# Adding the last chunk's rows to the token tiles: by an accumulating DMA in DRAM, or by 0/1 products on TensorE

## The reference, cut to what matters

```python
flat = layernorm(x)                      # 1250 x 1024
for e in range(8):
    cw = sum(where(topk_idx == e, topk_w, 0))
    y = gelu(flat @ w1[e].T + b1[e]) @ w2[e].T + b2[e]
    out = out + y * cw[:, None]          # only tokens that chose e have cw != 0
out = out + flat
x = x + (out - mean(out)) * rsqrt(var(out) + 1e-12) * ln_w + ln_b
```

## Time and profile before

| | us |
|---|---|
| median of 3 runs | 615.42 |
| the profiled execution: its own time | 617.8 |
| its span, first to last instruction | 615.7 |
| TensorE busy | 533.8 (87%) |
| VectorE busy | 464.7 (75%) |
| ScalarE busy | 243.0 (39%) |
| GpSimd busy | 194.4 (32%) |
| mean granted TensorE clock | 0.954 of full |

### The profile page before, as it was taken

The page is one execution under the profiler, slowest core; times in us unless marked ns, Lnnn a source line. Parts: engine busy times, 40 slices in busy tenths (PEclk is TensorE's granted clock), DMA queues, the critical chain, the costliest instruction groups (busy, mean ns, idle before and its releaser), DMA issues.

```text
span 615.7 us, 12330 instructions
## 1 busy us (share of the span) xinstructions
PE 533.8 (87%) x3660; PEld 298.8 (49%) x3661; DVE 464.7 (75%) x1295; ACT 243.0 (39%) x358; POOL 194.4 (32%) x199
## 2 busy tenths in 40 slices
PE   1799999899999999995879999999999999999100
PEld 1344554445544555553764655556565656564000
DVE  8889869996185888888748678695868685755397
ACT  5334444323271434342634343444443444401480
POOL 3023000000001375746434535343453444151240
PEclk9999999999999999997789999999999999999755
DMA  6873531243237334346367959698888889273878
GB/s 237 322 289 100 155 89 25 56 78 65 50 140 271 137 139 172 138 171 204 90 262 203 296 164 256 217 238 274 208 251 207 258 230 281 29 168 77 264 209 278
DMA packets 59581, 112.34 MB, mean 182 GB/s; under 512 B 33506, under 2 KB 33919, under 8 KB 59520
## 3 DMA queue, kind: packets, MB, share of 16 engines
q1 hardware_dynamic: 49440, 80.02, 37.4%
q0 software_dynamic: 8896, 27.38, 21.3%
q10 hardware_dynamic: 1184, 4.20, 1.9%
HBM read 71.75 MB, written 33.67 MB: 171 GB/s over the span
## 4 chain that ended last, share of the span: by engine, by line
PE 77%; DVE 14%; issue 4%; DMA 3%; ACT 1%; DVEq 0%; ACTq 0%; SPq 0%; POOLq 0%
PE ps L1818 7%; PE ps L1819 7%; PE ps L1943 7%; PE ps L1944 6%; PE ps L1945 6%; PE ps L1922 6%; PE ps L1923 5%; PE ps L1924 5%; PE ps L1728 5%; PE ps L1729 4%; PE ps L1730 4%; PE ps L1655 4%; PE ps L1904 4%; DMA acc_rows<-work,ids_out 1%; DVE wbufs L1574 1%
## 5 line engine op out<-in xcount | busy, mean ns | idle before, releaser
L615 POOL DMA_INDIRECT acc_rows<-work,ids_out x24 | 53.0, 2206 | 107.6 <-DVE work L1510 107.6
L1922 PE MATMUL ps<-rows_and_counts,wbufs 128*128 128x336 f16 (+2 forms) x256 | 76.1, 301 | 3.0 <-issue 2.2
L1924 PE MATMUL ps<-rows_and_counts,wbufs 128*128 128x336 f16 (+2 forms) x256 | 76.1, 301 | 0.0
L1923 PE MATMUL ps<-rows_and_counts,wbufs 128*128 128x336 f16 (+2 forms) x256 | 76.1, 301 | 0.0
L1819 PE MATMUL ps<-wbufs,rows_and_counts 128*128 128x512 f16 x200 | 75.8, 379 | 0.0
L1818 PE MATMUL ps<-wbufs,rows_and_counts 128*128 128x512 f16 x200 | 75.8, 379 | 0.0
L1943 PE MATMUL ps<-wbufs,rows_and_counts 128*128 (+1 forms) x192 | 72.9, 380 | 1.8 <-issue 1.3
L1465 DVE SCALAR_TENSOR_TENSOR wbufs<-stage,wbufs 128x1024 f16<-128x1024 f32 x56 | 67.1, 1218 | 8.1 <-ACT wbufs L933 7.6
L1944 PE MATMUL ps<-wbufs,rows_and_counts 128*128 (+1 forms) x192 | 72.8, 379 | 0.0
L1945 PE MATMUL ps<-wbufs,rows_and_counts 128*128 (+1 forms) x192 | 72.8, 379 | 0.0
L528 POOL TENSOR_TENSOR work<-work 128x1024 f16<-128x1024 f32 x9 | 19.2, 2132 | 164.3 <-ACT work L906 164.3
(11 more groups left out here) (310 smaller groups left out, 1050.5 us busy)
## 6 DMA issues: line engine op xcount, KB each, us to landing
stage<-wst_in SPq DMA_DIRECT2D x72, 512.0 KB
acc_rows<-work SPq DMA_DIRECT2D x10, 512.0 KB
x_rows<-work SPq DMA_DIRECT2D x10, 512.0 KB
wbufs<-b_in ACTq DMA_DIRECT2D x8, 512.0 KB
wbufs<-acc_rows SPq DMA_DIRECT2D x8, 512.0 KB, 5.9
t<-x_in SPq DMA_DIRECT2D x1, 3584.0 KB, 13.2
t<-x_in SPq DMA_DIRECT2D x1, 3072.0 KB, 11.3
t<-x_in SPq DMA_DIRECT2D x1, 2048.0 KB, 7.8
```

What stands on the lines that cost most here:

```text
L1922: mm(o, wbufs[:, ds(w + ws, P)], x_hi, start=(j == 0), stop=False)
L1923: mm(o, wbufs[:, ds(w + ws, P)], x_lo, start=False, stop=False)
L1924: ins = mm(o, wbufs[:, ds(w + (LO + ws), P)], x_hi, start=False, stop=(j == DK - 1))
```

## The change

The last chunk is taken out of the DRAM sum. Every token tile is loaded from `acc_rows` as soon as the adds of the chunk before the last have landed, and the last chunk's rows are put on top in PSUM.

- GpSimd, in the chunk before the last, makes a row of token numbers 384 to 1663 (`iota` of 128 x 1280, fp16) before it copies the next chunk's row ids; after that chunk there are no more adds to `acc_rows`.
- VectorE, at the start of the last chunk (`hot_tokens`), makes three 128 x 1280 fp16 matrices that are 1 where a row's id is the token's number.
- For each of the last chunk's six results VectorE reads it with the bias (L1506 as before), ScalarE makes its weighted fp16 high part (`last_hi`), and VectorE makes the low part from the weighted value less the high part (`last_lo`). The old L1510 is not run in this chunk.
- TensorE (`onto`) adds sub-chunks to token tiles: for tile r, sub-chunk i and half n, two products of 512 columns (0/1 matrix by high part and by low part). Tile 0 takes sub-chunk 0 and is made between k = 3 and k = 4 of `down`; tile 1 takes sub-chunks 0 and 1, tiles 2 to 9 all three. Four PSUM pairs of banks are used in turn.
- VectorE (`add_last`) adds the PSUM tile to `fin[r]` and sums the row in the same instruction; ScalarE takes the squares of all ten tiles. `bn_stats`, ScalarE's Copy with a sum, `last_ends` and `needs` go.
- Groups are (0,1), (2,3,4), (5,6,7), (8,9). Tiles 0 to 7 go out by ScalarE's scaling and GpSimd's adding DMA (before: 0 to 3); `t` of tiles 4 to 7 is stored early behind the `fin` loads. Tiles 8 and 9 are finished by VectorE and stored.

```diff
-LAST_GROUPS = (0, 1, 2, 3), (4, 5, 6, 7), (8, 9)
-ACT_TILES = (0, 1), (4, 5), (8,)
-ADDED = LAST_GROUPS[0]
-WHOLE = LAST_GROUPS[1] + LAST_GROUPS[2]
+LAST_GROUPS = (0, 1), (2, 3, 4), (5, 6, 7), (8, 9)
+STORED_1, STORED_2 = (0, 1, 2, 3), (4, 5, 6, 7)
+WHOLE = LAST_GROUPS[-1]
...
+                if before_last:
+                    pool.wait_ge(x4_done, DK * c + 2 * DK)
                     settle(pool)
+                    g.iota(token_row, [[1, NP]], base=CH, channel_multiplier=0,
+                           allow_small_or_imprecise_dtypes=True).then_inc(token_row_done, 1)
+                pool.wait_ge(cw_copied, c + 1)
+                settle(pool)
+                chunk_ids(c + 1, ids_weights)
+                if before_last:
+                    pool.sem_inc(last_ids_done, 1)
+                gather_weights(ids_weights)
...
-            pool.wait_ge(out_stored, 16 * len(ADDED))
-            for r in ADDED:
+            pool.wait_ge(out_stored, 16 * len(STORED_1))
+            for r in STORED_1 + STORED_2:
+                if r == STORED_2[0]:
+                    pool.wait_ge(out_stored2, 16 * len(STORED_2))
                 pool.wait_ge(scaled, r + 1)
                 g.indirect_dma_start(out=out, ...
...
-            sp.wait_ge(needs_done, 1)
+            sp.wait_ge(last_adds, 1)
             for r in range(NT):
-                sp.wait_ge(last_adds, sp.value_load(needs[0:1, r:r + 1], min_val=1, max_val=CT + 1))
-                settle(sp)
                 sp.dma_start(fin[r], acc_rows[CH + r * P:CH + (r + 1) * P, :]).then_inc(fin_in[r], 16)
+            for r in STORED_2:
+                sp.dma_start(out[r * P:(r + 1) * P, :], t[:, r * D:(r + 1) * D]).then_inc(out_stored2, 16)
...
                 if last:
+                    act.wait_ge(cw_copied, c + 1)
+                    for k in range(2 * CT):
+                        i, n = k // 2, k % 2
+                        act.wait_ge(down_read, c * (2 * CT) + (k + 3))
+                        a.activation(last_hi[:, i * D + n * HALF:i * D + (n + 1) * HALF], y_out[i][:, n * HALF:(n + 1) * HALF],
+                                     ACT.Copy, scale=cw_chunk[:, i * NE + e:i * NE + e + 1]).then_inc(last_hi_done, 1)
                     return
...
+            def square_of(r):
+                act.wait_ge(summed, r + 1)
+                st5.link(a.activation(minus5[:, r:r + 1], sum5[:, r:r + 1], ACT.Copy, scale=-1.0 / D))
+                a.activation(junk[r % 2], fin[r], ACT.Square, bias=minus5[:, r:r + 1],
+                             accum_out=square5[:, r:r + 1]).then_inc(squared, 1)
...
+            for r in range(NT):
+                square_of(r)
+                for n, tiles in enumerate(LAST_GROUPS[:-1]):
+                    if r == min(tiles[-1] + 2, NT - 1):
+                        std_of(n)
+                    if r == tiles[-1] + 3:
+                        scale_of(n)
+            std_of(len(LAST_GROUPS) - 1)
+            scale_of(len(LAST_GROUPS) - 2)
...
+            def hot_tokens():
+                dve.wait_ge(last_ids_done, 1)
+                for i in range(CT):
+                    st5.did(v.tensor_copy(last_ids_f[i], ids_weights[:, i:i + 1]))
+                st5.wait()
+                dve.wait_ge(token_row_done, 1)
+                for i in range(CT):
+                    v.tensor_scalar(token_hot[:, i * NP:(i + 1) * NP], token_row, last_ids_f[i], None, ALU.is_equal
+                                    ).then_inc(token_hot_done, 1)
+
+            def add_last(r):
+                dve.wait_ge(fin_in[r], 16)
+                dve.wait_ge(onto_done, r + 1)
+                v.scalar_tensor_tensor(fin[r], token_ps[r % 4], 1.0, fin[r], ALU.mult, ALU.add,
+                                       accum_out=sum5[:, r:r + 1]).then_inc(summed, 1)
...
+                        if last:
+                            at = slice(i * D + n * HALF, i * D + (n + 1) * HALF)
+                            dve.wait_ge(last_hi_done, k + 1)
+                            v.scalar_tensor_tensor(last_lo[:, at], o, cw_chunk[:, i * NE + e:i * NE + e + 1], last_hi[:, at],
+                                                   ALU.mult, ALU.subtract).then_inc(last_lo_done, 1)
+                            if k == 2 * CT - 2:
+                                add_last(0)
+                            continue
...
+            add_last(1)
+            for r in range(NT):
+                if r + 2 < NT:
+                    add_last(r + 2)
+                for n, tiles in enumerate(LAST_GROUPS):
+                    if r == tiles[-1]:
+                        var_of(n)
+                weigh(r)
+                for n, tiles in enumerate(LAST_GROUPS):
+                    if r == tiles[-1] + 1:
+                        rstd_of(n)
+            rstd_of(len(LAST_GROUPS) - 1)
...
+            def onto(r, tiles, start=True, stop=True):
+                for i in tiles:
+                    for n in range(2):
+                        pe.wait_ge(last_lo_done, 2 * i + n + 1)
+                        o = token_ps[r % 4][:, n * HALF:(n + 1) * HALF]
+                        hot = token_hot[:, i * NP + r * P:i * NP + (r + 1) * P]
+                        at = slice(i * D + n * HALF, i * D + (n + 1) * HALF)
+                        mm(o, hot, last_hi[:, at], start=(start and i == tiles[0]), stop=False, skip_group_check=True)
+                        ins = mm(o, hot, last_lo[:, at], start=False, stop=(stop and i == tiles[-1]), skip_group_check=True)
+                return ins
...
             down(c_last, half_of(c_last), True)
+            onto(1, (0, 1)).then_inc(onto_done, 1)
+            onto(2, (0, 1), stop=False)
+            onto(2, (2,), start=False).then_inc(onto_done, 1)
+            for r in range(3, NT):
+                if r == 3:
+                    pe.wait_ge(down_read, c_last * (2 * CT) + (2 * CT + 2))
+                else:
+                    pe.wait_ge(summed, r - 3)
+                onto(r, range(CT)).then_inc(onto_done, 1)
```

More of the change, by code:

```diff
@@ L284, in build @@
         shift5 = cw2[:, 6 * NT:7 * NT]
+        token_hot = stage[:, 2 * D:].bitcast(F16)[:, 0:CT * NP]
+        token_row = rows16[:, 2 * CT * D:2 * CT * D + NP]
+        last_hi, last_lo = [rows16[:, i * CT * D:(i + 1) * CT * D] for i in range(2)]
+        last_ids_f = tile_no[:, 0:1], tile_min[:, 0:1], tile_max[:, 0:1]
+        junk = gx[2], counts[:, CT * D:(CT + 1) * D]
         e_hi = [w[:, 0:PIECES * D] for w in (wbuf0, wbuf1)]
@@ L321, in build @@
         down_ps = [bank(6), bank(7)]
+        token_ps = [bank(2 * i, 2) for i in range(4)]
         act_step5 = sem("act_step5")
@@ L358, in build @@
         edges_in = sem("edges_in")
-        finished = sem("finished")
+        last_hi_done = sem("last_hi_done")
         first_done = sem("first_done")
@@ L590, in _, with chunk @@
             c_last = pool.value_load(last_chunk[:], min_val=NE - 1, max_val=MAXC - 3)
-            def chunk(c, ahead=None, last=False):
+            def chunk(c, ahead=None, last=False, before_last=False):
                 if isinstance(c, int):
@@ L637, in _ @@
                 chunk(last_2, gx)
-            chunk(last_1)
+            chunk(last_1, before_last=True)
             chunk(c_last, last=True)
@@ L1001, in _, with std_of, scale_of @@
             st5 = Steps(act, act_step5)
[L1002 to L1015, removed]
-            for n, tiles in enumerate(LAST_GROUPS):
-                cs = slice(tiles[0], tiles[-1] + 1)
+            def square_of(r):
[3 more added lines that the diff above has]
+                             accum_out=square5[:, r:r + 1]).then_inc(squared, 1)
+            def std_of(n):
+                cs = slice(LAST_GROUPS[n][0], LAST_GROUPS[n][-1] + 1)
                 act.wait_ge(var5_done, n + 1)
                 a.activation(std5[:, cs], var5[:, cs], ACT.Sqrt).then_inc(std5_done, 1)
-                if n + 1 < len(ACT_TILES):
-                    sums_of(n + 1)
-                if tiles[0] not in ADDED:
-                    continue
+            def scale_of(n):
                 act.wait_ge(rstd5_done, n + 1)
-                for r in tiles:
+                for r in LAST_GROUPS[n]:
                     act.wait_ge(weighed, r + 1)
                     a.activation(fin[r], fin[r], ACT.Copy, scale=rstd5[:, r:r + 1]).then_inc(scaled, 1)
+            for r in range(NT):
[7 more added lines that the diff above has]
+            scale_of(len(LAST_GROUPS) - 2)
         @block.vector
@@ L1365, in place @@
                     st3.link(v.tensor_tensor(cnt[:], cnt[:], first_slot[0:1, :], ALU.subtract))
-                    st3.did(v.tensor_copy(last_ends[:, r:r + 1], cnt[0:1, NE - 1:NE]))
                 else:
@@ L1371, in place @@
                         st3.link(v.tensor_scalar(carry[:, 0:1], carry[:, 0:1], float(FIRST_CH), None, ALU.max))
-                    st3.did(v.tensor_scalar(last_ends[:, r:r + 1], carry[0:1, NE - 1:NE], -float((NE - 1) * CAP * P), None,
-                                            ALU.add))
```

(19 more changed lines are left out.)

84 lines of the change are left out of this document (28 added, 56 removed).

## The result

The changed kernel takes 624.2 us (median of 4 runs, 623.45 to 626.65), against 615.13 for the kernel before in the same comparison (613.46 to 615.75): a ratio of 1.0152, with a 95% interval from 1.0121 to 1.0182, so 9 us slower. The forecast was 618.1 us, with a range up to 620.9: the direction was right, the size was not, and the time lies outside the range. The profiled execution took 624.12 us; its span is 622.4.

The account below looks back on a forecast made before the run. It took the DMA engines to bound the new tail: full from 598.5 for 18.8 us, until 617.3, plus 1.1 gives span 618.4, 2.7 above 615.7, so median 618.1 us. Own range 616.1 to 620.1; 8 in 10: 614.3 to 620.9.

Parts of the forecast that it names:

- Ids, iota, 0/1 matrices and loads hidden: Front of the tail: iota 1.2 to 1.55 us, comparisons and copies at most 4 us, inside VectorE's 7.0 us idle time.
- The path from `down` to `add_last`: TensorE and VectorE up to 576.4: high and low parts take 2.1 us per result, within 2.59; last low part at 576.4.
- TensorE never slow before tile 9: TensorE in the tail: 2.59 us per tile from tile 3, full clock, no long idle time, tile 9 done at 595.9.
- VectorE: VectorE's list in the tail: 1.35 us per add with sum (1.2 to 1.5), 1.2 per multiply-add, tile 9 finished at 607.3.
- The adds: GpSimd's adds to the output: issued from 588, then 596.6, last at 608.5; 2.7 us of the DMA engines each.
- The last packet: End of DMA work: engines full from 598.5 with six adds and two stores, 18.8 us, until 617.3.
- The step that failed: End of the kernel: span ends 1.1 us after the last packets, as before, so 617.3 + 1.1 = 618.4 us.
- the last add was not spared by the others: Rival at the output: last add lands 5.8 us after issue, at 614.3, unslowed by other adds; median 615.1; chance 0.18.
- VectorE did not end the kernel: Rival at the end: VectorE's last tile, at 607.3 plus 3.4 us, ends the kernel; median 610.4; chance 0.04.
- the clock did not fall early: Rival in the tail: TensorE at its lower clock from tile 3, 18 us more, median about 634; chance 0.04.
- nothing held up the last chunk: Rival in the front: `hot_tokens` or late loads delay the last chunk by 1 to 4 us; median 619 to 622; chance 0.05.

Follow-up runs that it names:

- The first experiment: Kernel before, with GpSimd also waiting for all stores to the output before it ends: 624.39 us against 616.74, ratio 1.0124.
- the second experiment: Changed kernel with the last wait for the eight adds moved from GpSimd to SyncE: 625.47 us against 616.74, ratio 1.0134.
- the pair with five adds: Changed kernel with tiles 5 to 7 finished by VectorE and stored by SyncE: 616.51 us with SyncE waiting for the adds, 618.65 with GpSimd waiting.

## Why the prediction was wrong, point by point

- **Ids, iota, 0/1 matrices and loads hidden**: right. The iota took 1.78 us (1.2 to 1.55 forecast), the comparisons 0.55 us (at most 1.2), and 4.54 us of idle time were left. The loads were issued from 547.9 on, 551.3 in the frame of before (554.8 forecast).
- **The path from `down` to `add_last`**: right. The last low part was ready at 573.0, in the frame of before 576.4, as forecast. ScalarE's 128 x 512 took 0.72 us, not the 0.55 taken from the earlier trace rows, still within the pitch.
- **TensorE never slow before tile 9**: right; nothing like the earlier trace rows came, the granted clock was 1.00 in 586 to 594, in which its products ended, and in 594 to 596.
- **VectorE**: an `add_last` took 1.22 us from start to start of the next, where 1.35 was taken between 1.2 and 1.5; VectorE ended at 606.1 in the frame of before, 607.3 forecast. The Trainium skill ("VectorE: DVE Perf Modes", section "Two Vector instructions with no wait between them") counts such an operation as two instructions, and the trace agrees in form: a read of 0.08 us stands behind each. It costs next to nothing: from start to start an `add_last` takes 1.22 us with its read, and the multiply-add behind it 1.19 (586.43 to 587.62).
- **The adds**: issued at 588.4, 595.8 and, last, 607.8 in the frame of before, against 588, 596.6 and 608.5. Right within 0.8 us, as is the price of 2.7 us in the stretch that decides.
- **The last packet**: forecast 617.3, 60.4 us after the first product of `down`; measured 614.2, 60.8 us after its own. All the working up to here was off by 0.4 us. A little of that is luck: the third add was issued 0.8 us earlier than forecast, but its packets began 2.9 us behind its issue and not 1.9, so the start of the full stretch, 598.7 in the frame of before against 598.5, came out right by two misses.
- **The step that failed** is the one behind it: "and the span ended at 615.7, 1.1 us later. So the new span is 617.3 + 1.1". The description of the kernel before has the same gap where it says that the program ends when the stores and the adds have landed. That 1.1 us is what stands behind a store that SyncE waits for. Behind an add that GpSimd waits for stands its closing DRAIN: from last add packet to end it was 615.7 - 607.6 = 8.1 us before, hidden beside the last stores, and is 8.2 us after, exposed. The forecast let the last work pass from one engine to another and kept the price of the first engine's ending. With 8.1 in place of 1.1 the sum gives 617.3 + 8.1 - 615.7 = 9.7 us more span and a median of 625.1, against 624.2 measured. The first experiment shows the 7 us by themselves. The 8.1 us are 0.6 from the last packet to the end of the wait, 7.3 of DRAIN and 0.2 until the last instruction.
- **The rivals**: the last add was not spared by the others (landings up to 10.3 us; the forecast of full engines held); VectorE did not end the kernel; the clock did not fall early; nothing held up the last chunk. The cause was among none of them, and the range, drawn from bounds of terms that were all right, left it out.
- **Could it be seen before?** Yes: in the row of L107 shown above. With the adds landed at 608 and the DRAIN at 7.3 us, the kernel before was already ended by GpSimd's DRAIN, 0.3 us behind SyncE, so any delay of the last add was bound to reach the end in full. Indeed 60.8 - 50.7 = 10.1 us, the delay of the last add packet in the tail, is the whole 10.1 us by which the tail grew.

What stays open: what the DRAIN does in its 7.3 us, and why it is 4.3 when it begins before the adds have landed. All kernels here issue indirect DMAs on GpSimd, so whether the DRAIN would be as long without any is not shown. The saving of 3.5 us of tail in the second experiment was seen in one trace each, and the medians do not confirm it; the pair with five adds (2.1 us in both views) is the better evidence that the place of the wait counts.

## What to carry to other kernels

Before you price a new end of a kernel, look past the last packet: ask which engine waits for it and what that engine's ending costs, in the rows of the program's last line, since neither the busy times nor the chain of waits show it. Let GpSimd be done early, and let SyncE wait for its DMAs: here that took 2.1 to 3.5 us off a tail that GpSimd's DRAIN had ended clearly last, and nothing that is certain off one where it had not. And count what an accumulating DMA costs the engines against a plain one, here 2.7 against 1.3 us per 512 KB, before moving a sum there that an engine could do.

## What the runs showed of the hardware

- GpSimd's closing DRAIN takes 7.2 to 7.4 us once its last wait is over (7341, 7422, 7177 ns), whether it had waited for adds, plain writes or another engine's stores; behind a sum of its own it ended 7.5 us after the sum. Begun with adds outstanding it ends 4.2 to 4.4 us after their last packet (four kernels). SyncE's takes 13 ns.
- An indirect DMA that adds a 128 x 1024 fp32 tile in DRAM takes 2.7 to 3.0 us of all 16 engines, one that writes it 1.3; issue on GpSimd 1.5 to 2.3 against 0.96 to 1.72 us; median landing, one behind the other, 6.9 against 4.1 us.
- A 128 x 1024 fp32 sum on GpSimd takes 2.3 us where VectorE does little and 2.9 beside its wide operations. VectorE's operations on two SBUF tiles stretch from 1.28 to 3.4 us beside it, its read of PSUM does not; an operation of 128 x 3 with one tile as input took 1.18 us there and 0.17 elsewhere.
- The time until the last chunk's `down` differed from one execution to the next by up to 7 us (552.7 to 559.9, over several chips; by 4.8, 555.1 and 559.9, on one) in kernels whose front is the same; two traces are to be laid over each other at a common instruction before a few microseconds are read out of them.
